# One of four key tiles of the value product as three fp32r passes of a split pair, q projected one unit ahead

## Chip, core and metric

The kernel runs on one core of a Trainium2 chip. The metric is the device time of one execution in microseconds; a shorter time is better. Engines: TensorE (PE, with its weight loads PEld), VectorE (DVE), ScalarE (ACT), GpSimd (POOL) and SyncE (SP), which issues DMAs here.

## The reference

Four layers on x of 2048 tokens by 256: a recurrent time mix, an FFN with low-rank experts, an attention, and an FFN with one of eight experts. Each adds to x what it computes from a layer norm of x. The change is in the attention, 16 heads of 128:

```python
w = codes * jnp.repeat(scales, block_size, axis=0)      # q, k, v, out
q = _mxfp4_matmul(x, wq_codes, wq_scales) + bq
...
scores = jnp.einsum('bqhd,bkhd->bhqk', q, k) / jnp.sqrt(jnp.float32(HEAD_DIM))
attn = jax.nn.softmax(scores, axis=-1)
out = jnp.einsum('bhqk,bkhd->bqhd', attn, v).reshape(B, S, NUM_HEADS * HEAD_DIM)
return _mxfp4_matmul(out, wo_codes, wo_scales) + bo
```

## The kernel before

attention() works on units: a unit u is a head (u // 4) and a block of 512 query tokens (u % 4), 64 units in all. Each unit has four steps c = 0 to 3, and each step takes four key tiles of 128 (KPC = 4, 16 key tiles in all). Every engine runs its own list of instructions over the same steps s = 4u + c, written out by hand, and semaphores tie them together. In step s:

- TensorE: score (L1212), four tiles of keys against 512 queries, each as three fp32r passes (hi by hi, hi by lo, lo by hi; the helper three, L574 to L578); turn_top and spread_top (c = 0) for the maximum of each query; project for q (c = 1), for k (all steps of the last unit of a head); sum_rows (c = 2); weigh (L1241 to L1253), the value product of the step PV = 6 earlier, four tiles, each one fp32 matmul, which the profile records as two instructions; project_out (c = 2, 3); project_v, the values of two heads, in four steps out of 32.
- ScalarE: keep (L1321) copies scores from PSUM to prob, in two halves of two tiles, exp (L1327) of the step SUB = 5 earlier; widen_top (L1333) at c = 0; out_hi (L1340) and project_hi (L1312).
- VectorE: shift (L1380) subtracts the maximum in psum_m from prob, of the step 5 earlier, in two halves; largest (L1390, L1393) keeps the running maximum of the scores; row_max (L1404) at c = 0, fold_top (L1397) at c = 3; project_lo (L1372), out_lo (L1414), the reciprocals (L1410), two output adds (L1426) at c = 2 and 3, take_v (L1435).
- GpSimd: add_up sums the probabilities into acc2, at c = 0 of the summed unit in one operation (L1488), else in two (L1492, L1495), with a last fold at c = 3 (L1500). It sums the step that ScalarE has just exponentiated. It also splits weights into hi and lo (split, L1060 to L1064).
- SyncE loads the next weights as soon as the buffers are split.

The lo part of a value is the value less its hi part, where hi is the value as fp32r. Projections come back through two banks psum_w, in the order of the table jobs; claim() waits until the job two before is taken. The order of VectorE in a step is: shift of half 0, out_lo (c = 2), shift of half 1, largest of half 0, row_max (c = 0), largest of half 1, fold_top (c = 3), project_lo, the reciprocals, the output adds, take_v. That of ScalarE is: out_hi (c = 2), keep and exp of half 0, keep and exp of half 1, widen_top (c = 0), project_hi.

## Time and profile before

| | us |
|---|---|
| median of 3 runs | 2996.99 |
| lowest, highest run | 2992.41, 3002.51 |
| the profiled execution's own time | 2983.7 |
| its span | 2982.0 |
| PE busy | 2791.7 (94%) |
| DVE busy | 1974.7 (66%) |
| ACT busy | 1298.6 (44%) |
| POOL busy | 1454.5 (49%) |

Busy time is the time in which an engine has an instruction in work. Matmuls overlap, so the pace of TensorE is the distance between starts and not the mean of one. The attention runs from about 600 to 2679 us.

### The profile page before, as it was taken

What the parts mean: (1) busy time and instruction counts of PE and PEld (TensorE: products, weight loads), DVE (VectorE), ACT (ScalarE), POOL (GpSimd) and SP (SyncE); (2) the same over time, 40 slices, a digit from 0 to 9 for tenths busy, and PEclk for the clock granted to TensorE, in tenths of its full rate; (3) what the DMA queues carried; (4) which work ended last, traced back from release to release, by engine and by line L of the source; (5) the groups of instructions that cost most, each with busy time, mean ns of one, the idle gap of its engine ahead of it and who ended that gap; (6) DMA issues with size and microseconds to landing.
All of it is one profiled execution on the core that took longest, in us unless ns stands there. A gap on an engine that the chain in (4) does not pass through costs nothing. (4 is left out here: it accounts for less than half of the span.)

```text
span 2982.0 us, 31410 instructions
## 1 busy us (share of the span) xinstructions
PE 2791.7 (94%) x10874; PEld 1856.1 (62%) x10875; DVE 1974.7 (66%) x2412; ACT 1298.6 (44%) x1557; POOL 1454.5 (49%) x782
## 2 busy tenths in 40 slices
PE   5886899889999999999999999999999999987995
PEld 2232677566666667667666766766676676657663
DVE  4478443567777777787777777777777777764211
ACT  1201321245555555555555555455545545541121
POOL 0022230046666666665665666567666655664002
PEclk9888699999999999999999999999999999997997
DMA  2000100110000000000000000000000000006012
GB/s 63 0 0 1 49 0 0 22 27 10 11 8 13 8 4 20 4 8 8 13 9 3 20 8 4 8 13 11 3 9 8 4 1 4 1 10 244 23 44 78
DMA packets 57717, 57.71 MB, mean 19 GB/s; under 512 B 8336, under 2 KB 52624, under 8 KB 57584
## 3 DMA queue, kind: packets, MB, share of 16 engines
q1 hardware_dynamic: 54944, 48.75, 6.1%
q0 software_dynamic: 2640, 7.21, 0.7%
q8 instruction: 80, 1.31, 0.2%
q14 instruction: 53, 0.43, 0.0%
HBM read 45.72 MB, written 10.22 MB: 19 GB/s over the span
## 5 line engine op out<-in xcount | busy, mean ns | idle before, releaser
L1251 PE MATMUL at_psum_o<-at_prob,at_v 128*128 128x512 f32 x2048 | 925.6, 595 | 0.0
L1321 ACT ACTIVATE at_prob<-at_psum_s 128x1024 f32<-128x1024 f32 x512 | 523.6, 1023 | 801.8 <-PE at_psum_s L578 801.8
L1492 POOL TENSOR_TENSOR at_acc<-at_acc,at_prob 128x1024 f32<-128x1024 f32 x192 | 454.7, 2368 | 516.7 <-ACT at_prob L1327 516.4
L1380 DVE TENSOR_TENSOR at_prob<-at_prob,at_psum_m 128x1024 f32<-128x1024 f32 x512 | 604.8, 1212 | 65.4 <-PE at_psum_m L1238 65.4
L1393 DVE TENSOR_TENSOR at_top<-at_psum_s,at_top 128x1024 f32<-128x1024 f32 x448 | 547.2, 1221 | 104.9 <-ACT at_prob L1321 92.3
L1251 PEld LDWEIGHTS at_psum_o<-at_prob,at_v 128*128 128x128 f32 x2048 | 379.2, 190 | 380.4 <-issue 367.8
L1327 ACT ACTIVATE at_prob<-at_prob 128x1024 f32<-128x1024 f32 x512 | 539.0, 1053 | 13.2 <-DVE at_prob L1380 12.9
L1495 POOL TENSOR_TENSOR at_acc<-at_acc,at_prob 128x1024 f32<-128x1024 f32 x192 | 475.0, 2474 | 28.1 <-POOL at_acc L1492 0.9
L576 PE MATMUL at_psum_s<-at_q_hi,at_k_hi 128*128 128x512 f32 x1024 | 429.9, 420 | 2.2 <-DVE at_k_lo L1372 2.2
L578 PE MATMUL at_psum_s<-at_q_hi,at_k_lo 128*128 128x512 f32 x1024 | 402.1, 393 | 0.0
L577 PE MATMUL at_psum_s<-at_q_lo,at_k_hi 128*128 128x512 f32 x1024 | 401.4, 392 | 0.0
L1488 POOL TENSOR_TENSOR at_acc<-at_prob 128x1024 f32<-128x1024 f32 x64 | 151.6, 2369 | 208.6 <-ACT at_prob L1327 207.2
L1426 DVE SCALAR_TENSOR_TENSOR x_tok<-at_psum_w,at_rsum,x_tok 128x256 f32<-128x256 f32 x256 | 112.1, 479 | 178.3 <-PE at_psum_w L578 178.3
L576 PEld LDWEIGHTS at_psum_s<-at_q_hi,at_k_hi 128*128 128x128 f32 x1024 | 192.6, 188 | 50.4 <-DVE at_q_lo L1372 8.8
L577 PEld LDWEIGHTS at_psum_s<-at_q_lo,at_k_hi 128*128 128x128 f32 x1024 | 192.7, 188 | 46.8 <-issue 13.6
L578 PEld LDWEIGHTS at_psum_s<-at_q_hi,at_k_lo 128*128 128x128 f32 x1024 | 192.2, 188 | 44.0
L418 POOL TENSOR_TENSOR tm_read<-tm_r,tm_state 128x2048 f32<-128x2048 f32 x8 | 33.3, 4160 | 217.7 <-DVE tm_state L438 217.7
L576 PE MATMUL at_psum_w<-at_wo_hi,at_oT_hi 128*128 128x256 f32 x256 | 122.9, 480 | 0.0
L576 PE MATMUL at_psum_w<-at_x_hi,at_w_hi 128*128 128x512 f32 x256 | 103.0, 402 | 4.3 <-PEq L62 4.3
L916 ACT ACTIVATE lf_hidden<-lf_psum_h,lf_b 128x512 f32<-128x512 f32 x64 | 41.0, 685 | 146.8 <-PE lf_psum_h L578 146.8
L578 PE MATMUL at_psum_w<-at_x_hi,at_w_lo 128*128 128x512 f32 x256 | 101.8, 398 | 0.0
L577 PE MATMUL at_psum_w<-at_x_lo,at_w_hi 128*128 128x512 f32 x256 | 101.3, 396 | 0.0
(314 smaller groups left out, 3889.0 us busy)
## 6 DMA issues: line engine op xcount, KB each, us to landing
ef_gate_up<-in_ef_gate_up SPq DMA_DIRECT2D x8, 1024.0 KB, 14.0
ef_down<-in_ef_down SPq DMA_DIRECT2D x8, 512.0 KB, 12.7
ef_rows_in<-ef_zeros SPq DMA_DIRECT2D x23, 128.0 KB, 1.8
ef_rows<-ef_rows_in SPq DMA_DIRECT2D x23, 128.0 KB, 2.0
ef_rows_out<-ef_result POOLq DMA_DIRECT2D x23, 128.0 KB, 2.0
x_tok<-in_L_attn_x SPq DMA_DIRECT2D x1, 2048.0 KB, 8.2
lf_w<-in_L_ffn_W SPq DMA_DIRECT2D x2, 1024.0 KB, 6.8
at_codes<-in_at_wq_codes SPq DMA_DIRECT2D x16, 128.0 KB, 2.1
```

What stands on the lines that cost most here:

```text
L576: nc.tensor.matmul(out, a_hi, b_hi, start=start, stop=False, **kw)
L577: nc.tensor.matmul(out, a_hi, b_lo, start=False, stop=False, **kw)
L578: return nc.tensor.matmul(out, a_lo, b_hi, start=False, stop=stop, **kw)
L1251: last = nc.tensor.matmul(psum_o[:], v[:, kt, half], prob[u % 2][:, kt, :], start=(kt == 0), stop=(kt == KT - 1))
L1321: nc.scalar.activation(prob[u % 2][:, c * KPC + 2 * half:c * KPC + 2 * half + 2, :], psum_s[:, 2 * half:2 * half + 2, :], ACT.Copy).then_i ...
L1327: nc.scalar.activation(part, part, ACT.Exp).then_inc(exp_done, 1)
L1380: nc.vector.tensor_tensor(part, part, psum_m[:].unsqueeze(1).to_broadcast([P, 2, BT]), ALU.subtract).then_inc(shifted, 1)
L1393: nc.vector.tensor_tensor(top2[:], part, top2[:], ALU.max).then_inc(maxed, 1)
L1426: last = nc.vector.scalar_tensor_tensor(row, bank(key)[:, bass.ts(j, D)], rsum[:, u % 2, t:t + 1], row, ALU.mult, ALU.add)
L1488: nc.gpsimd.tensor_tensor(acc2[:], first, second, ALU.add).then_inc(summed, 2)
L1492: nc.gpsimd.tensor_tensor(acc2[:], acc2[:], first, ALU.add).then_inc(summed, 1)
L1495: nc.gpsimd.tensor_tensor(acc2[:], acc2[:], second, ALU.add).then_inc(summed, 1)
```

## The change

- The last of the four key tiles of each step (SPLIT = 1, KF = 3) is multiplied as three fp32r passes, with v_hi, v_lo as weights and p_hi, p_lo streamed. The other three stay fp32.
- p_hi is made by ScalarE (split_hi, a copy of 512 columns of prob to fp32r), p_lo by VectorE (split_lo, prob less p_hi), both 256 times. weigh waits for p_lo before its last tile.
- take_v makes v_whole, v_hi and v_lo for that tile, from 256 columns each.
- widen_top goes: spread_top reads a column of row_top with a step of zero as weights.
- q is projected for the next unit (c = 1) instead of for the next head; its buffers hold two blocks. Two q projections move from the first three steps to units 1 and 2.
- The weights of q and k are loaded and split apart, with a semaphore each. The lists of loads on SyncE are reordered: k, v, o, q. GpSimd splits k at step 2 of a head and q at step 10, where it split both at 2.

The diff, cut to its core:

```diff
+SPLIT = 1
...
+    KF = KPC - SPLIT
...
-        if c == 1 and u >= 1 and u - 1 < U - NB:
-            job(("q", (u - 1) // NB + 1, (u - 1) % NB))
+        if c == 1 and u + 1 < U:
+            job(("q", *divmod(u + 1, NB)))
         if s < 3:
             job(("k", 0, s + 1))
-            job(("q", 0, s + 1))
...
+        def split_q(pool, h):
+            pool.wait_ge(qk_loaded[0], (h + 1) * N_QK)
             if h >= 1:
                 pool.wait_ge(w_ready, jobs["q", h - 1, NB - 1] + 1)
-                pool.wait_ge(w_ready, jobs["k", h - 1, NB - 1] + 1)
             nc.gpsimd.tensor_tensor(scales[:, 0], scales[:, 0], factor[:].unsqueeze(2).to_broadcast([P, NC, HD]),
                                     ALU.mult).then_inc(q_factor, 1)
             pool.wait_ge(q_factor, h + 2)
-            split(pool, w_hi[:], codes[:], scales[:], w_lo[:], w_split, h * 3)
+            split(pool, w_hi[:, 0], codes[:, 0], scales[:, 0], w_lo[:, 0], w_split[0], h * 3)
+
+        def split_k(pool, h):
+            pool.wait_ge(qk_loaded[1], (h + 1) * N_QK)
+            if h >= 1:
+                pool.wait_ge(w_ready, jobs["k", h - 1, NB - 1] + 1)
+            split(pool, w_hi[:, 1], codes[:, 1], scales[:, 1], w_lo[:, 1], w_split[1], h * 3)
...
                     for h in range(NH):
...
+                        if h + 1 < NH:
+                            sp.wait_ge(w_split[1], (h + 1) * 3)
+                            load_qk(sp, 1, h + 1)
+                        if h % 2 == 0 and h // 2 + 1 < NH // 2:
+                            sp.wait_ge(wv_split, (h // 2 + 1) * 3)
+                            load_v(sp, h // 2 + 1)
+                        if h >= 1:
+                            sp.wait_ge(wo_split, h * 3)
+                            load_o(sp, h)
+                        if h + 1 < NH:
+                            sp.wait_ge(w_split[0], (h + 1) * 3)
+                            load_qk(sp, 0, h + 1)
...
-                            last = nc.tensor.transpose(psum_m[:, bass.ts(t, P)], wide_top[:, t, :], ident[:])
+                            last = nc.tensor.transpose(psum_m[:, bass.ts(t, P)], row_top[:, t:t + 1].to_broadcast([P, P]), ident[:])
...
-                            last = nc.tensor.matmul(psum_o[:], v[:, kt, half], prob[u % 2][:, kt, :],
-                                                    start=(kt == 0), stop=(kt == KT - 1))
+                            nc.tensor.matmul(psum_o[:], v[:, c, t, half], prob[u % 2][:, c * KPC + t, :],
+                                             start=(c == 0 and t == 0), stop=False)
+                        pe.wait_ge(p_lo_ready, u * CH + c + 1)
+                        slot = (u * CH + c) % 2
+                        for t in range(SPLIT):
+                            last = three(nc, psum_o[:], v_hi[:, c, t, half], v_lo[:, c, t, half],
+                                         p_hi[:, slot, t, :], p_lo[:, slot, t, :],
+                                         start=False, stop=(c == CH - 1 and t == SPLIT - 1))
...
-                    def widen_top(u):
...
+                    def split_hi(u, c):
+                        n = u * CH + c
+                        act.wait_ge(exp_done, 2 * n + 2)
+                        if n >= 2:
+                            act.wait_ge(pv_done, n - 1)
+                        nc.scalar.activation(p_hi[:, n % 2], prob[u % 2][:, c * KPC + KF:(c + 1) * KPC, :],
+                                             ACT.Copy).then_inc(p_hi_ready, 1)
...
+                    def split_lo(u, c):
+                        n = u * CH + c
+                        dve.wait_ge(p_hi_ready, n + 1)
+                        if n >= 2:
+                            dve.wait_ge(pv_done, n - 1)
+                        nc.vector.tensor_tensor(p_lo[:, n % 2], prob[u % 2][:, c * KPC + KF:(c + 1) * KPC, :],
+                                                p_hi[:, n % 2].bitcast(F32), ALU.subtract).then_inc(p_lo_ready, 1)
...
+                            nc.vector.tensor_tensor(v_whole[:, 0:2 - plain, :], psum[:, plain:2, :], wide,
+                                                    ALU.add).then_inc(v_steps, 1)
+                            nc.vector.tensor_tensor(v_hi[:, c, part, :], psum[:, plain:2, :], wide,
+                                                    ALU.add).then_inc(v_steps, 1)
+                            dve.wait_ge(v_steps, m + 2)
+                            made = nc.vector.tensor_tensor(v_lo[:, c, part, :], v_whole[:, 0:2 - plain, :],
+                                                           v_hi[:, c, part, :].bitcast(F32), ALU.subtract)
...
                         if at == 2 and h + 1 < NH:
-                            split_qk(pool, h + 1)
+                            split_k(pool, h + 1)
+                        if at == 10 and h + 1 < NH:
+                            split_q(pool, h + 1)
```

How this moves instructions, at three places of the middle of the attention. VectorE in the steps c = 0 and c = 1 of a unit before: shifts (at_prob), running maxima (at_top), row_max (at_row_top), project_lo (at_q_lo).

```order
L1380 TENSOR_TENSOR at_prob<-at_prob,at_psum_m 128x1024 x2
L1390 COPY at_top<-at_psum_s 128x1024 [waits at_top_ready,at_kept]
L1404 TENSOR_REDUCE at_row_top<-at_psum_w 128x4 [waits at_wide_ready,at_w_ready]
L1393 TENSOR_TENSOR at_top<-at_psum_s,at_top 128x1024 [waits at_maxed,at_kept]
L1380 TENSOR_TENSOR at_prob<-at_prob,at_psum_m 128x1024 [waits at_top_spread]
L1380 TENSOR_TENSOR at_prob<-at_prob,at_psum_m 128x1024
L1393 TENSOR_TENSOR at_top<-at_psum_s,at_top 128x1024 [waits at_maxed,at_kept] x2
L1372 SCALAR_TENSOR_TENSOR at_q_lo<-at_psum_w,at_bias,at_q_hi 128x512 [waits at_hi_ready]
L1380 TENSOR_TENSOR at_prob<-at_prob,at_psum_m 128x1024
```

The same steps of VectorE now:

```order
L1398 TENSOR_TENSOR at_prob<-at_prob,at_psum_m 128x1024 x2
L1408 COPY at_top<-at_psum_s 128x1024 [waits at_top_ready,at_kept]
L1422 TENSOR_REDUCE at_row_top<-at_psum_w 128x4 [waits at_top_spread,at_w_ready]
L1411 TENSOR_TENSOR at_top<-at_psum_s,at_top 128x1024 [waits at_maxed,at_kept]
L1453 TENSOR_TENSOR at_p_lo<-at_prob,at_p_hi 128x512 [waits at_pv_done,at_p_hi_ready]
L1398 TENSOR_TENSOR at_prob<-at_prob,at_psum_m 128x1024 [waits at_top_spread]
L1398 TENSOR_TENSOR at_prob<-at_prob,at_psum_m 128x1024
L1411 TENSOR_TENSOR at_top<-at_psum_s,at_top 128x1024 [waits at_maxed,at_kept] x2
L1390 SCALAR_TENSOR_TENSOR at_q_lo<-at_psum_w,at_bias,at_q_hi 128x512 [waits at_hi_ready]
L1453 TENSOR_TENSOR at_p_lo<-at_prob,at_p_hi 128x512 [waits at_pv_done,at_p_hi_ready]
L1398 TENSOR_TENSOR at_prob<-at_prob,at_psum_m 128x1024
```

A subtraction into at_p_lo with two waits has come to the end of each step, behind row_max and the maxima at c = 0 and behind project_lo at c = 1; before, the next step's shift followed there.

ScalarE in the same two steps before: keep (at_prob from at_psum_s), exp (at_prob from at_prob), widen_top, project_hi (at_q_hi).

```order
L1321 ACTIVATE at_prob<-at_psum_s 128x1024 [waits at_scored]
L1327 ACTIVATE at_prob<-at_prob 128x1024 [waits at_shifted]
L1333 ACTIVATE at_wide_top<-at_row_top 128x512 [waits at_top_spread,at_w_free]
L1321 ACTIVATE at_prob<-at_psum_s 128x1024 [waits at_scored,at_summed,at_pv_done]
L1327 ACTIVATE at_prob<-at_prob 128x1024 [waits at_shifted]
L1321 ACTIVATE at_prob<-at_psum_s 128x1024 [waits at_scored]
L1327 ACTIVATE at_prob<-at_prob 128x1024 [waits at_shifted]
L1312 ACTIVATE at_q_hi<-at_psum_w,at_bias 128x512 [waits at_w_ready]
L1340 ACTIVATE at_oT_hi<-at_psum_o 128x512 [waits at_w_ready,at_pv_done]
```

ScalarE there now:

```order
L1339 ACTIVATE at_prob<-at_psum_s 128x1024 [waits at_scored]
L1345 ACTIVATE at_prob<-at_prob 128x1024 [waits at_shifted]
L1352 ACTIVATE at_p_hi<-at_prob 128x512 [waits at_pv_done,at_exp_done]
L1339 ACTIVATE at_prob<-at_psum_s 128x1024 [waits at_scored,at_summed,at_pv_done]
L1345 ACTIVATE at_prob<-at_prob 128x1024 [waits at_shifted]
L1339 ACTIVATE at_prob<-at_psum_s 128x1024 [waits at_scored]
L1345 ACTIVATE at_prob<-at_prob 128x1024 [waits at_shifted]
L1352 ACTIVATE at_p_hi<-at_prob 128x512 [waits at_pv_done,at_exp_done]
L1330 ACTIVATE at_q_hi<-at_psum_w,at_bias 128x512 [waits at_w_ready]
L1359 ACTIVATE at_oT_hi<-at_psum_o 128x512 [waits at_w_ready,at_pv_done]
```

The copy into at_wide_top is gone, and a copy into at_p_hi follows the second exp of each step; at c = 1 project_hi stands behind it.

TensorE in weigh and the first spreading transpose at c = 0, before:

```order
L1251 MATMUL at_psum_o<-at_prob,at_v 128x512 [waits at_exp_done]
L1251 MATMUL at_psum_o<-at_prob,at_v 128x512
L1251 MATMUL at_psum_o<-at_prob,at_v 128x512 [waits at_exp_done]
L1251 MATMUL at_psum_o<-at_prob,at_v 128x512
L1238 MATMUL at_psum_m<-ident,at_wide_top 128x128 [waits at_shifted,at_wide_ready]
```

TensorE there now:

```order
L1264 MATMUL at_psum_o<-at_prob,at_v 128x512 [waits at_exp_done]
L1264 MATMUL at_psum_o<-at_prob,at_v 128x512
L1264 MATMUL at_psum_o<-at_prob,at_v 128x512 [waits at_exp_done]
L576 MATMUL at_psum_o<-at_p_hi,at_v_hi 128x512 [waits at_p_lo_ready]
L577 MATMUL at_psum_o<-at_p_lo,at_v_hi 128x512
L578 MATMUL at_psum_o<-at_p_hi,at_v_lo 128x512
L1252 MATMUL at_psum_m<-ident,at_row_top 128x128 [waits at_shifted,at_w_free]
```

The fourth fp32 tile has become three passes, the first of which waits for p_lo, and the transpose waits for row_max itself (at_w_free) instead of the copy.

## Rows read from the trace of the kernel before

**Rows 1.** Busy time by stretch: a unit, the attention; clock, DMA, GB/s last
```profile
core 0: us, PE busy (x) PEld busy (x) DVE busy (x) ACT busy (x) POOL busy (x), PEclk, DMA share, GB/s
1501.00:1530.40 29.40, 29.40 (x117) 19.32 (x116) 23.31 (x25) 17.02 (x19) 21.16 (x13) 1.00 0.11 18
700.00:2300.00 1600.00, 1600.00 (x6551) 1085.68 (x6550) 1224.50 (x1341) 874.53 (x996) 1005.96 (x504) 1.00 0.04 9
```

**Rows 2.** Timeline of TensorE, start and duration in us
```profile
1512.24 3.59 PE L1251 MATMUL at_psum_o<-at_prob,at_v 128*128 128x512 f32 x8
1515.27 0.80 PE L576 MATMUL at_psum_s<-at_q_hi,at_k_hi 128*128 128x512 f32 x1
1515.91 0.40 PE L577 MATMUL at_psum_s<-at_q_lo,at_k_hi 128*128 128x512 f32 x1
...
1523.48 0.40 PE L576 MATMUL at_psum_s<-at_q_hi,at_k_hi 128*128 128x512 f32 x1
...
1526.24 3.59 PE L1251 MATMUL at_psum_o<-at_prob,at_v 128*128 128x512 f32 x8
```

**Rows 3.** Groups by form, VectorE then ScalarE, 700 to 2300 us
```profile
L1380 DVE TENSOR_TENSOR at_prob<-at_prob,at_psum_m 128x1024 f32<-128x1024 f32 x398 | 470.3, 1212 | 50.9 <-PE at_psum_m L1238 50.9
L1393 DVE TENSOR_TENSOR at_top<-at_psum_s,at_top 128x1024 f32<-128x1024 f32 x348 | 425.0, 1221 | 77.4 <-ACT at_prob L1321 67.8
L1426 DVE SCALAR_TENSOR_TENSOR x_tok<-at_psum_w,at_rsum,x_tok 128x256 f32<-128x256 f32 x198 | 86.7, 479 | 139.2 <-PE at_psum_w L578 139.2
...
L1372 DVE SCALAR_TENSOR_TENSOR at_q_lo<-at_psum_w,at_bias,at_q_hi 128x512 fp32r<-128x512 f32 x50 | 37.5, 751 | 15.0 <-ACT at_q_hi L1312 15.0
L1414 DVE TENSOR_TENSOR at_oT_lo<-at_psum_o,at_oT_hi 128x512 fp32r<-128x512 f32 x50 | 34.5, 690 | 27.9 <-ACT at_oT_hi L1340 27.9
L1404 DVE TENSOR_REDUCE at_row_top<-at_psum_w 128x4 f32<-128x512 f32 x49 | 33.3, 679 | 0.0
...
L1410 DVE RECIPROCAL at_rsum<-at_psum_w 128x4 f32<-128x4 f32 x50 | 8.6, 172 | 0.0
...
L1333 ACT ACTIVATE at_wide_top<-at_row_top 128x512 f32<-128x512 f32 x49 | 30.8, 628 | 0.0
```

**Rows 4.** Timelines of ScalarE, GpSimd and VectorE around one step
```profile
1526.07 1.05 ACT L1327 ACTIVATE at_prob<-at_prob 128x1024 f32<-128x1024 f32 x1
...
1527.92 1.06 ACT L1327 ACTIVATE at_prob<-at_prob 128x1024 f32<-128x1024 f32 x1
...
1513.73 2.37 POOL L1488 TENSOR_TENSOR at_acc<-at_prob 128x1024 f32<-128x1024 f32 x1 [2.74 <-ACT at_prob L1327]
...
1527.20 2.37 POOL L1492 TENSOR_TENSOR at_acc<-at_acc,at_prob 128x1024 f32<-128x1024 f32 x1 [1.69 <-ACT at_prob L1327]
1529.71 2.68 POOL L1495 TENSOR_TENSOR at_acc<-at_acc,at_prob 128x1024 f32<-128x1024 f32 x1
...
1529.33 0.79 DVE L1397 TENSOR_TENSOR at_top<-at_top 128x512 f32<-128x512 f32 x1
```

**Rows 5.** Timelines: fold_top alone, then with an add
```profile
633.06 0.69 DVE L1397 TENSOR_TENSOR at_top<-at_top 128x512 f32<-128x512 f32 x1
...
1330.90 0.69 DVE L1397 TENSOR_TENSOR at_top<-at_top 128x512 f32<-128x512 f32 x1
...
1330.94 2.92 POOL L1495 TENSOR_TENSOR at_acc<-at_acc,at_prob 128x1024 f32<-128x1024 f32 x1
```

**Rows 6.** Timelines of VectorE and GpSimd in the first layer's scan
```profile
217.16 4.42 DVE L438 TENSOR_TENSOR_SCAN tm_state<-tm_decay,tm_kv 128x2048 f32<-128x2048 f32 x1
...
224.97 5.49 DVE L438 TENSOR_TENSOR_SCAN tm_state<-tm_decay,tm_kv 128x2048 f32<-128x2048 f32 x1
...
221.67 4.51 POOL L418 TENSOR_TENSOR tm_read<-tm_r,tm_state 128x2048 f32<-128x2048 f32 x1 [6.17 <-DVE tm_state L438]
```

**Rows 7.** TensorE's timeline and a stretch at the attention's end
```profile
2673.96 1.84 PE L1260 MATMUL at_psum_w<-at_ones,at_acc 128*128 128x1 f32 x8 [3.52 <-POOL at_acc L1500]
...
2674.00:2678.00 4.00, 4.00 (x19) 4.00 (x20) 0.85 (x3) 0.00 (x0) 0.00 (x0) 0.50 0.00 0
```

More of the change, by code:

```diff
@@ L1158, in attention @@
             halves = {key: n for n, key in enumerate(k for k in jobs if k[0] in "qk")}
+            split_jobs = [n for n in range(KT // 2) if 2 * n % KPC + 2 > KF]
+            v_split_jobs = len(split_jobs)
+            v_split_index = {n: i for i, n in enumerate(split_jobs)}
             def bank(key):
@@ L1354, in _ @@
                                 exp(eu, ec, half)
-                        if c == 0 and 1 <= u <= U:
-                            widen_top(u - 1)
-                        if c == 1 and u >= 1 and u - 1 < U - NB:
-                            project_hi(0, (u - 1) // NB + 1, (u - 1) % NB)
+                        if 0 <= eu < U:
+                            split_hi(eu, ec)
+                        if c == 1 and u + 1 < U:
+                            project_hi(0, *divmod(u + 1, NB))
                         if s < 3:
                             project_hi(1, 0, s + 1)
-                            project_hi(0, 0, s + 1)
                         if u % NB == NB - 1 and u < U - 1:
@@ L1459, in _ @@
                                 fold_top(u)
-                        if c == 1 and u >= 1 and u - 1 < U - NB:
-                            project_lo(0, (u - 1) // NB + 1, (u - 1) % NB)
+                        if c == 1 and u + 1 < U:
+                            project_lo(0, *divmod(u + 1, NB))
                         if s < 3:
                             project_lo(1, 0, s + 1)
-                            project_lo(0, 0, s + 1)
                         if u % NB == NB - 1 and u < U - 1:
                             project_lo(1, u // NB + 1, c)
+                        if 0 <= eu < U:
+                            split_lo(eu, ec)
                         if c == 2 and 2 <= u < U + 2:
```

102 lines of the change are left out of this document (47 added, 55 removed).

## The prediction

> **What bounds the kernel now.** I read the busy time by stretch first, then TensorE's timeline, then VectorE's groups, then the three other engines around one step. From 700 to 2300 us TensorE is busy 1600 of 1600 us at granted clock 1.00 [rows 1]: the attention is its stage. A unit (one head, 512 query tokens, four steps) without projections of keys or values takes 29.4 us, in which VectorE is busy 23.31 and GpSimd 21.16. I call it a plain unit. Its timeline gives the passes. Twelve fp32r passes of a score step run from 1523.48 to 1526.24, 0.230 each; the eight records of four fp32 tiles run from 1512.24 to one pass before 1515.91, 3.44 us, or 0.86 a tile [rows 2].
>
> **TensorE: what is removed.** One tile of each of 256 steps goes from 0.86 to 3 x 0.230 = 0.69, so 0.17 x 256 = 43 us of work go, and a plain unit would need 28.7. [...]
>
> Around it: q projections keep their number; two of them (1.4 us each) move from the first steps, where TensorE waited for k_lo, into steps where it doesn't, and half of that comes back, +1.4 us. widen_top leaves ScalarE; the spreading transposes read row_top with a zero step. No row has such a weight load; ScalarE read the same broadcast in 0.63 us [rows 3], no longer than VectorE takes for 512 columns (0.69), so I take 0, and at worst a few tenths for 64 units. The weight loads of q and k are split into two visits of SP and GpSimd with the same bytes; q's DMAs now stand behind the wait for the o split on SP and have over ten steps before they are used: 0.
>
> **ScalarE and VectorE: what is added.** 256 split_hi of 512 columns, 0.63 each like widen_top [rows 3], put ScalarE from 17 to about 19 us of a unit: hidden. 256 split_lo on VectorE: unhindered, 0.69 [rows 5], less 0.08 that neighbours overlap. Four make VectorE's own work 23.3 + 2.5 = 25.8; with its waits for ScalarE in step c = 1 and for kept halves I count 27.3. That alone still fits under 28.7. Of every second value bank one tile is split: its take becomes four operations of 256 columns, about 0.4 each (the 256-column output adds take 0.48 [rows 3]), so a value step has 0.69 + 1.6 = 2.3 us on VectorE, where TensorE has 2.9 us of projection.
>
> **What split_lo collides with.** It reads two SBUF operands (prob and p_hi), and GpSimd's adds read two as well. The trace of before has three such meetings. fold_top (top2 with top2) takes 0.69 alone [rows 5], but 0.79 when it starts 0.24 us before L1492 ends (1527.20 + 2.37 = 1529.57) [rows 4]. A GpSimd add started 0.04 after it takes 2.92 instead of 2.37 [rows 5]. The scan of the first layer takes 4.42 alone and 5.49 when it starts 1.21 before GpSimd's product ends (221.67 + 4.51) [rows 6]. Each time the second operation is held for what is left of the first, less 0.14. Shifts and maxima, which have one operand in PSUM, keep 1.21 and 1.22 whatever GpSimd does [rows 3]. The Trainium skill (SBUF — State Buffer, Who interferes with whom) says that a VectorE instruction with two SBUF inputs and a GpSimd instruction that reads SBUF exclude each other, the later one for the whole of the earlier; the trace agrees up to a hold of 1.07 us, and has none longer.
>
> So the phase decides. In step c = 3 exp0 starts at 1526.07, L1492 at +1.13, L1495 at +3.64; exp1 ends at 1528.98, +2.91 [rows 4]. split_hi ends near +3.6, when L1495 starts. VectorE has a row_max, a fold or an out_lo ahead of split_lo in three of four steps and comes later than that: it finds GpSimd at the start of a 2.37 us add.
>
> **The walk**, in us from the first shift of a step, once VectorE is the late one from the durations of [rows 3, 4]: shifts to 2.34; exp0 1.29 to 2.34; L1492 2.42 to 4.8; L1495 4.93 to 7.3; maxima to 4.82; exp1 to 4.2; p_hi at 4.95.
> - c = 0: row_max puts the end of the maxima at 5.4; split_lo held until 7.3, done 7.85; next shift 7.8.
> - c = 1: GpSimd has one add here, 0.13 after exp1 (like the one at 1513.73), 4.37 to 6.74. project_hi now stands behind split_hi, so project_lo ends at 6.4; split_lo done 7.3; 7.25.
> - c = 2: out_lo between the shifts; split_lo from 5.55 held to 7.3, done 7.85; reciprocal and two adds of output rows to 8.8.
> - c = 3: fold holds L1495 until about 7.8; it waits already when fold ends at 5.56, so split_lo is held until 7.8, done 8.4; two output adds, 9.2.
>
> Sum 33.05, where VectorE without holds has 27.3 and TensorE 28.7. The next unit begins alike, so it is the period: +3.65 on 29.4. Behind it TensorE becomes the waiting engine, first at spread_top, which waits for row_max, and at score, which waits for the maxima.
>
> Units: 64, of which 15 carry k projections. There TensorE has 5.6 us more, project_lo fits into the held time, and both need 34 to 35: +0.5 each, +8. Seven carry a pair of heads' values: VectorE has about 2.3 us more in each of four steps, TensorE 2.9: +2 each, +14. That leaves 41 plain ones (one is the fill): 41 x 3.65 = +150. The tail has no scores to hide split_hi and split_lo: +4, with the fill's 1.4, +5. Sum +177. The TensorE work removed (43) is inside these, since the new period is VectorE's. 2983.7 + 177 = 3161 for the profiled execution; the median of the runs shown is 13.3 above it, so I forecast **3174 us**, 6% slower.
>
> The bounds: if no hold is longer than the longest seen, 1.07, the holds are 1.07 + 0.25 + 1.07 + 1.07 = 3.5 and the unit 30.8, +1.4 x 41 = +57: about 3054. If near ties go to VectorE in one step of four, its hold of 1.75 goes: 31.3, +1.9 x 41, with the rest 3100.
>
> **Rivals.**
> - *Faster: split_lo goes in ahead of the second add.* Place: the start of L1495 against the end of split_hi, some 0.1 us apart. If VectorE is there first, GpSimd is held for 0.5, which it can afford (21 of 29), nothing is held on VectorE, and TensorE stays the bound: -43 + 1.4 + 3 for the tail = -38, 2959. For it: in c = 2 the maxima end about when p_hi comes. Against: in c = 0 and c = 3 VectorE is busy until 0.4 and 0.7 after L1495's start, and two holds of 2 us already make 27.3 + 4 = 31.3 over 28.7. It decides only if holds stay under 28.7 - 27.3 = 1.4 us a unit. [...] Chance 0.12, with all other ways to no lasting hold.
> - *Holds end early*, capped at 1.07: 3054. Chance 0.06.
> - *TensorE's clock falls too.* In the walk TensorE waits some 3.4 us at spread_top in each unit. After the one wait of 3.52 us in the tail, the next 4 us ran at granted 0.50, the 1.2 GHz level [rows 7]. Were that so in each plain unit, up to 4 us of its work would take twice as long, and of the 4.3 us that TensorE has over, little is left: up to +2 x 41 = +80, 3255. Chance 0.04.
> - *No difference*: holds of just about 1.4 to 2 us a unit, which eat the 43 us: 0.02.
>
> **How the numbers follow.** The forecast case has 0.76. About 9 us, 0.3%, is what a measurement can tell from no change. Faster 0.12, same 0.02, slower 0.86. The forecast's own range is 3080 to 3230 (periods of 31.4 to 34.4 us); taking in the capped holds below and most of the clock case above gives 3040 to 3250, and leaves out the faster case and the rest, under 0.2.
>
> **What would show it.** split_lo's mean near 2 us instead of 0.69, with the short ones in the steps with the single add; VectorE near 95% busy in the attention where it had 77%; TensorE's busy share down, with waits for at_p_lo, row_top and maxima; a plain unit of 33 us. The forecast is wrong if split_lo averages under about 1.0 us, or if TensorE is still busy without gaps; its size is off if the hold is there but the phase of the adds another.

## The result: 4.6% slower, and the profile after

| | before | after |
|---|---|---|
| median of the runs, us | 2994.7 (4 runs, 2989.8 to 3002.5) | 3132.7 (4 runs, 3126.9 to 3140.2) |
| span of the profiled execution, us | 2982.0 | 3125.2 |

The ratio is 1.046, 95% interval 1.0431 to 1.049. The time is 41 us under the forecast of 3174 and inside the range. The busy shares and two stretches after, in the columns of [rows 1] (the attention, and a plain unit):

```profile
PE 2802.0 (90%) x11130; PEld 1932.3 (62%) x11131; DVE 2451.6 (78%) x2764; ACT 1444.6 (46%) x1749; POOL 1524.5 (49%) x830
...
700.00:2300.00 1600.00, 1512.96 (x6386) 1079.73 (x6385) 1503.61 (x1525) 931.91 (x1079) 993.39 (x503) 0.98 0.04 9
1588.00:1620.00 32.00, 31.70 (x118) 22.13 (x118) 29.36 (x29) 18.70 (x23) 20.97 (x12) 0.90 0.02 7
```

TensorE had no gap in the attention [rows 1]; now it is idle for 87 of 1600 us, and VectorE is busy 1504 of 1600, 94%, where it had 1224.5. The groups of VectorE and GpSimd for the same stretch, beside [rows 3]:

```profile
L1398 DVE TENSOR_TENSOR at_prob<-at_prob,at_psum_m 128x1024 f32<-128x1024 f32 x374 | 441.2, 1209 | 0.0
L1411 DVE TENSOR_TENSOR at_top<-at_psum_s,at_top 128x1024 f32<-128x1024 f32 x329 | 400.9, 1218 | 18.5 <-ACT at_prob L1339 4.2
L1453 DVE TENSOR_TENSOR at_p_lo<-at_prob,at_p_hi 128x512 fp32r<-128x512 f32 x187 | 365.8, 1956 | 0.4 <-ACT at_p_hi L1352 0.3
...
L1541 POOL TENSOR_TENSOR at_acc<-at_acc,at_prob 128x1024 f32<-128x1024 f32 x140 | 358.3, 2559 | 20.6 <-POOL at_acc L1538 0.9
L1538 POOL TENSOR_TENSOR at_acc<-at_acc,at_prob 128x1024 f32<-128x1024 f32 x141 | 337.9, 2397 | 441.8 <-ACT at_prob L1345 441.8
```

split_lo (L1453) takes 1.96 us in the mean for 512 columns, though an operation of that size takes 0.69 alone [rows 5]. The time over 0.69 I call its hold. Shifts and maxima, with one operand in PSUM, keep their 1.21 and 1.22. Shifts no longer wait for anything, where they had 50.9 us of waits for TensorE in [rows 3]. The timelines of VectorE's split_lo and fold_top and of GpSimd, over one plain unit (start and duration in us):

```profile
1588.99 2.66 DVE L1453 TENSOR_TENSOR at_p_lo<-at_prob,at_p_hi 128x512 fp32r<-128x512 f32 x1
...
1598.17 1.11 DVE L1453 TENSOR_TENSOR at_p_lo<-at_prob,at_p_hi 128x512 fp32r<-128x512 f32 x1
...
1604.90 0.69 DVE L1453 TENSOR_TENSOR at_p_lo<-at_prob,at_p_hi 128x512 fp32r<-128x512 f32 x1 [0.29 <-ACT at_p_hi L1352]
...
1612.18 0.81 DVE L1415 TENSOR_TENSOR at_top<-at_top 128x512 f32<-128x512 f32 x1
1612.91 2.89 DVE L1453 TENSOR_TENSOR at_p_lo<-at_prob,at_p_hi 128x512 fp32r<-128x512 f32 x1
```

```profile
1588.74 2.36 POOL L1541 TENSOR_TENSOR at_acc<-at_acc,at_prob 128x1024 f32<-128x1024 f32 x1
...
1596.36 2.37 POOL L1534 TENSOR_TENSOR at_acc<-at_prob 128x1024 f32<-128x1024 f32 x1 [3.57 <-ACT at_prob L1345]
...
1604.94 2.92 POOL L1541 TENSOR_TENSOR at_acc<-at_acc,at_prob 128x1024 f32<-128x1024 f32 x1
...
1612.58 2.67 POOL L1541 TENSOR_TENSOR at_acc<-at_acc,at_prob 128x1024 f32<-128x1024 f32 x1
```

Put the two side by side. At 1588.99 split_lo starts 0.25 after an add that ends at 1591.10; without a hold it would take 0.69, and it ends at 1591.65, so its work began at 1590.96, 0.14 before the add's end. At 1598.17 the single add has 0.56 left, and split_lo takes 1.11 = 0.69 + 0.42, again 0.14 less than what was left. At 1604.90 split_lo starts 0.04 ahead of the add: it takes 0.69, and the add pays (2.92). At 1612.91 the add itself had been held by fold_top, and split_lo is held for 2.2 us, twice the longest hold in the trace before. The whole trace goes by this: 222 of the 256 split_lo start inside a two-input operation of GpSimd, and each is held for what is left of it less 0.09 to 0.15 us (0.14 in 212 of them).

TensorE's waits from 700 to 2300 us (total, times, longest), and its timeline at the first wait of this unit:

```profile
PE at_psum_m L1252 <- DVE at_row_top L1422: 42.5, 17, 2.7
PE at_psum_w L576 <- DVE x_tok L1444: 18.6, 17, 2.5
PE at_psum_o L1264 <- DVE at_oT_lo L1432: 14.9, 16, 1.1
PE at_psum_w L576 <- DVE at_rsum L1428: 11.1, 6, 1.8
```

```profile
1587.99 1.12 PE L1252 MATMUL at_psum_m<-ident,at_row_top 128*128 128x128 f32 x4 [2.70 <-DVE at_row_top L1422]
1588.76 0.78 PE L576 MATMUL at_psum_s<-at_q_hi,at_k_hi 128*128 128x512 f32 x1
1589.34 0.63 PE L577 MATMUL at_psum_s<-at_q_lo,at_k_hi 128*128 128x512 f32 x1
1589.76 0.63 PE L578 MATMUL at_psum_s<-at_q_hi,at_k_lo 128*128 128x512 f32 x1
```

Everything it waits for comes from VectorE. After the wait of 2.70 us its passes start 0.42 apart instead of 0.23: half the clock, as in [rows 7] (granted 0.50 from 1588 to 1594 us). The granted clock of the unit is 0.90, that of the attention 0.98.

**The units.** I take a unit's length from one first maximum (L1408, before L1390) to the next. All 63 such lengths, and what lies around them, make up the 143.2 us between the two spans. In the last column stands the forecast for the same units.

| group | before, each | after, each | sum, us | forecast, us |
|---|---|---|---|---|
| 28 plain units | 29.39 | 12 of 32.8, 1 of 32.65, 15 of 30.8 to 31.5 | +72.1 | +102 |
| 14 k units | 34.96 | 33.3 | -22.4 | +7 |
| 7 pairs of units with values | 70.07 | 78.7 (40.8 + 37.9) | +60.7 | +40 |
| units 60 to 62 | 29.39, 27.95, 27.96 | 32.8 | +13.1 | +11 |
| units 0 to 3 | | | +2.1 | +8 |
| before the first (-1.1), behind the last maximum (+18.6) | | | +17.5 | +9 |

### The profile page after: what moved, and what is told of

It reads as the page before. It is cut to its first block and busy times, and to the rows that moved or that the text cites. A ratio compares the mean times of both kernels' runs of the same rounds, so it can differ in the third digit from the quotient of the medians.

```text
span 3125.2 us, 32974 instructions
## 1 busy us (share of the span) xinstructions
PE 2802.0 (90%) x11130; PEld 1932.3 (62%) x11131; DVE 2451.6 (78%) x2764; ACT 1444.6 (46%) x1749; POOL 1524.5 (49%) x830
## 5 line engine op out<-in xcount | busy, mean ns | idle before, releaser
L1538 POOL TENSOR_TENSOR at_acc<-at_acc,at_prob 128x1024 f32<-128x1024 f32 x192 | 459.7, 2394 | 587.9 <-ACT at_prob L1345 587.9
L1264 PE MATMUL at_psum_o<-at_prob,at_v 128*128 128x512 f32 x1536 | 709.9, 598 | 26.0 <-DVE at_oT_lo L1432 24.1
L1453 DVE TENSOR_TENSOR at_p_lo<-at_prob,at_p_hi 128x512 fp32r<-128x512 f32 x256 | 501.8, 1960 | 8.9 <-ACT at_p_hi L1352 8.6
L1541 POOL TENSOR_TENSOR at_acc<-at_acc,at_prob 128x1024 f32<-128x1024 f32 x192 | 492.8, 2567 | 28.1 <-POOL at_acc L1538 0.9
L1264 PEld LDWEIGHTS at_psum_o<-at_prob,at_v 128*128 128x128 f32 x1536 | 283.1, 190 | 287.8 <-issue 233.6
L576 PE MATMUL at_psum_s<-at_q_hi,at_k_hi 128*128 128x512 f32 x1024 | 416.6, 407 | 5.5 <-DVE at_k_lo L1390 5.0
L577 PE MATMUL at_psum_s<-at_q_lo,at_k_hi 128*128 128x512 f32 x1024 | 410.2, 401 | 0.0
L578 PE MATMUL at_psum_s<-at_q_hi,at_k_lo 128*128 128x512 f32 x1024 | 409.1, 400 | 0.0
L576 PEld LDWEIGHTS at_psum_s<-at_q_hi,at_k_hi 128*128 128x128 f32 x1024 | 198.9, 194 | 44.5 <-DVE at_k_lo L1390 6.5
L576 PE MATMUL at_psum_o<-at_p_hi,at_v_hi 128*128 128x512 f32 x256 | 202.7, 792 | 0.1
L1352 ACT ACTIVATE at_p_hi<-at_prob 128x512 fp32r<-128x512 f32 x256 | 161.7, 632 | 8.1
L418 POOL TENSOR_TENSOR tm_read<-tm_r,tm_state 128x2048 f32<-128x2048 f32 x8 | 33.3, 4161 | 217.6 <-DVE tm_state L438 217.6
L1444 DVE SCALAR_TENSOR_TENSOR x_tok<-at_psum_w,at_rsum,x_tok 128x256 f32<-128x256 f32 x256 | 111.4, 475 | 13.1 <-PE at_psum_w L578 7.6
```

The costliest lines, as they stand in the source:

```text
L576: nc.tensor.matmul(out, a_hi, b_hi, start=start, stop=False, **kw)
L577: nc.tensor.matmul(out, a_hi, b_lo, start=False, stop=False, **kw)
L578: return nc.tensor.matmul(out, a_lo, b_hi, start=False, stop=stop, **kw)
L1264: nc.tensor.matmul(psum_o[:], v[:, c, t, half], prob[u % 2][:, c * KPC + t, :], start=(c == 0 and t == 0), stop=False)
L1352: nc.scalar.activation(p_hi[:, n % 2], prob[u % 2][:, c * KPC + KF:(c + 1) * KPC, :], ACT.Copy).then_inc(p_hi_ready, 1)
L1453: nc.vector.tensor_tensor(p_lo[:, n % 2], prob[u % 2][:, c * KPC + KF:(c + 1) * KPC, :], p_hi[:, n % 2].bitcast(F32), ALU.subtract).then_i ...
```

## The experiments

Eleven more kernels ran, each beside runs of the kernel before, whose median was 2984.0 to 2984.8 us each time. Diffs are against the change. These medians of before lie 10 us under the 2994.7 of the table above, so I compare a run with the change by its ratio; the first four expectations in microseconds were written before that was known.

**1. The rest of the change alone.** SPLIT's tile goes back to fp32, with no hi and lo parts of probabilities and values. What stays is the order of projections and loads, and the spreading without widen_top.

```diff
-    KF = KPC - SPLIT
+    KF = KPC
...
-                            split_hi(eu, ec)
...
-                            split_lo(eu, ec)
```

> All of the change except the split tile: four fp32 tiles in weigh, no split_hi, split_lo or split values; q is projected one unit ahead, the loads are reordered, the spreading transposes read row_top with a zero step. Port theory and load theory: nothing of it costs, 2995 to 3002 us (the moved q projections +1.4). Rival that the reordering or the zero-step weight load is what costs: 3050 or more, with TensorE waiting at at_psum_m or for at_w_free.

Measured: 2987.2 us, ratio 1.001 (0.9999 to 1.0021), and TensorE busy 1600 of 1600 us. The rest is free, as the prediction had it, to 0.2%; the loss is the split tile's.

**2. split_lo left out.**

```diff
-                        pe.wait_ge(p_lo_ready, u * CH + c + 1)
+                        pe.wait_ge(p_hi_ready, u * CH + c + 1)
...
-                                          p_hi[:, slot, t, :], p_lo[:, slot, t, :],
+                                          p_hi[:, slot, t, :], p_hi[:, slot, t, :],
...
-                            split_lo(eu, ec)
```

> The change without split_lo: weigh waits for p_hi and streams it in place of p_lo, so the lo part of the probabilities is left out of the product. TensorE's passes, split_hi and the split values stay. Port theory and load theory: VectorE is back at 23.3 of a plain unit of 28.7 us, so the TensorE gain shows: 2950 to 2965. Rival that the passes on TensorE, its clock or ScalarE's work cost: stays over 3000.

Measured: 2943.7 us, ratio 0.9871 (0.9849 to 0.9894), and TensorE busy without a gap. So 40 us are to be had from the passes. split_lo costs the difference of the ratios, 1.046 to 0.987, or some 176 us.

**3. and 4. split_lo's second input, and GpSimd's inputs.** In one kernel split_lo becomes an operation of its size that reads one operand; in the other split_lo is whole and GpSimd's sums only write, so the row sums are left out.

```diff
-                        nc.vector.tensor_tensor(p_lo[:, n % 2], prob[u % 2][:, c * KPC + KF:(c + 1) * KPC, :],
-                                                p_hi[:, n % 2].bitcast(F32), ALU.subtract).then_inc(p_lo_ready, 1)
+                        nc.vector.tensor_reduce(p_lo[:, n % 2, 0], prob[u % 2][:, c * KPC + KF, :].unsqueeze(2), AX.X,
+                                                ALU.max).then_inc(p_lo_ready, 1)
```

> split_lo replaced by an operation of VectorE of the same 512 columns, the same place and the same waits, that reads one SBUF operand (a maximum over groups of one), so p_lo holds a copy of prob and the product is another. Port theory: about 0.7 us each, never held, GpSimd's adds at 2.37 to 2.40, a plain unit of 28.7 to 29.0, total 2950 to 2975. Load theory (256 more operations in VectorE's list and their waits for ScalarE are enough): 3100 to 3135, as with the change.

```diff
-                            nc.gpsimd.tensor_tensor(acc2[:], acc2[:], second, ALU.add).then_inc(summed, 1)
+                            nc.gpsimd.memset(acc2[:], 1.0).then_inc(summed, 1)
```

(and the same for the other three sums.)

> The change with split_lo whole, but GpSimd's adds of probabilities only write ones (the row sums are left out): no GpSimd instruction of the loop reads SBUF except the weight splits. Port theory: split_lo at 0.69 but for steps with weight splits (mean 0.7 to 0.8), total 2950 to 2965. Load theory: as with the change, 3100 to 3135, split_lo at 0.7 but VectorE without a pause.

Measured: 2954.5 us, ratio 0.9906 (0.9887 to 0.9926), and 2949.2 us, ratio 0.9877 (0.9858 to 0.9895). The group of split_lo in the first and in the second, with the second's sum and the first's:

```profile
L1453 DVE TENSOR_REDUCE at_p_lo<-at_prob 128x512 fp32r<-128x512 f32 x204 | 138.2, 677 | 5.0 <-ACT at_p_hi L1352 5.0
...
L1541 POOL TENSOR_TENSOR at_acc<-at_acc,at_prob 128x1024 f32<-128x1024 f32 x153 | 382.0, 2496 | 22.5 <-POOL at_acc L1538 0.9
```

```profile
L1453 DVE TENSOR_TENSOR at_p_lo<-at_prob,at_p_hi 128x512 fp32r<-128x512 f32 x203 | 148.3, 731 | 1.1 <-ACT at_p_hi L1352 0.8
...
L1541 POOL MEMSET at_acc<- 128x1024 f32 x152 | 144.8, 953 | 132.9 <-ACT at_prob L1345 132.2
```

One more VectorE operation per step, with all of its waits and in the same place, costs next to nothing in plain units (28.7 in the mean) and 11 us in all against experiment 2: what costs is that it reads two operands in SBUF beside GpSimd operations that read. The second kernel's sums are also shorter, so alone it would show less than the first does.

**5. Preparations kept, the tile in fp32** (it reads the values of the step's first tile, so the product is another).

```diff
-                            last = three(nc, psum_o[:], v_hi[:, c, t, half], v_lo[:, c, t, half],
-                                         p_hi[:, slot, t, :], p_lo[:, slot, t, :],
-                                         start=False, stop=(c == CH - 1 and t == SPLIT - 1))
+                            last = nc.tensor.matmul(psum_o[:], v[:, c, 0, half], prob[u % 2][:, c * KPC + KF + t, :],
+                                                    start=False, stop=(c == CH - 1 and t == SPLIT - 1))
```

> The change with all preparations (split_hi, split_lo, split values, the wait for p_lo), but the fourth tile multiplied as one fp32 matmul with the weights of tile 0 of the step (p_hi, p_lo and the split values are not used). It takes TensorE's saving away: 43 us of passes come back. Port theory: where VectorE sets the period the time hardly moves; value steps and steps with k projections gain or lose a little: 3130 to 3155. Rival that TensorE is still the bound and lost time by other means: 43 us more, 3170 to 3180.

Measured: 3136.0 us, ratio 1.0514 (1.0496 to 1.0531), split_lo at 1.93 us. The ratio is 0.5% over the change's 1.046, some 16 us, where 43 us of work would be 1.4%: with VectorE as the bound, most of what TensorE saves is worth nothing.

**6. split_lo on GpSimd**, behind its own adds, in the same step.

```diff
-                        nc.vector.tensor_tensor(p_lo[:, n % 2], prob[u % 2][:, c * KPC + KF:(c + 1) * KPC, :],
+                        nc.gpsimd.tensor_tensor(p_lo[:, n % 2], prob[u % 2][:, c * KPC + KF:(c + 1) * KPC, :],
```

> split_lo moved to GpSimd, behind its adds of the same step; nothing left out. About 1.3 us each there. GpSimd goes from 18 to 23.4 us of a plain unit of 28.7. Port theory: VectorE is held only at fold_top, TensorE is the bound again in plain units: 2955 to 2975, with some waits for p_lo where GpSimd splits weights of values and outputs in one step (5 to 6 us of it). Load theory of VectorE: the same sign. Rival that p_lo comes too late from GpSimd: 3000 and more, waits of TensorE for at_p_lo.

Measured: 2989.9 us, ratio 1.0009 (0.9994 to 1.0024). The expected 2955 to 2975 missed. split_lo takes 1.29 us there, most plain units are at 28.67, and still nothing is won. TensorE's waits from 700 to 2300 us name one thing, six times; then GpSimd's timeline ahead of one of them:

```profile
PE at_psum_o L576 <- POOL at_p_lo L1521: 19.1, 6, 3.2
```

```profile
926.40 1.31 POOL L1521 TENSOR_TENSOR at_p_lo<-at_prob,at_p_hi 128x512 fp32r<-128x512 f32 x1
927.67 1.27 POOL L1064 TENSOR_TENSOR at_wv_hi<-at_v_codes,at_v_scales 128x512 fp32r<-128x512 f32 x1
...
933.72 2.41 POOL L1536 TENSOR_TENSOR at_acc<-at_acc,at_prob 128x1024 f32<-128x1024 f32 x1
...
939.93 1.26 POOL L1521 TENSOR_TENSOR at_p_lo<-at_prob,at_p_hi 128x512 fp32r<-128x512 f32 x1
```

Between two rest parts lie six weight splits (927.67 to 933.76), since at step 8 of every second head GpSimd splits the values' and the outputs' weights together. The rest part comes late, TensorE waits 3.2 us for it, and such units take 32 to 35 us. I had expected these waits, but put 5 to 6 us of GpSimd's work on them and not 3.2 us of TensorE's waiting six times over, with units longer by 3.5 to 6.

**7. split_lo on VectorE one step later**, right behind the second shift.

```diff
+                        if 0 <= pu < U:
+                            split_lo(pu, pc)
...
-                        if 0 <= eu < U:
-                            split_lo(eu, ec)
```

> split_lo stays on VectorE, whole, but one step later, right behind the second shift, some 2.3 us into the step, when GpSimd's second add of the step before is over and its first of this step is about to start; nothing left out. Port theory: mostly no hold, split_lo 0.69 to 1.0 in the mean, GpSimd's first add held by up to 0.5, total 2955 to 2985. Load theory (the work and not the phase): 3100 or more, since VectorE has exactly the work of the change.

Measured: 3043.6 us, ratio 1.0198 (1.0181 to 1.0215), a miss: I had expected at most 2985. Both groups of two-input operations on VectorE, 700 to 2300 us:

```profile
L1453 DVE TENSOR_TENSOR at_p_lo<-at_prob,at_p_hi 128x512 fp32r<-128x512 f32 x193 | 188.9, 979 | 0.0
L1415 DVE TENSOR_TENSOR at_top<-at_top 128x512 f32<-128x512 f32 x49 | 139.2, 2840 | 1.7
```

split_lo is nearly free now, but fold_top, with 0.72 in the change, takes 2.84. At 1524.48 it starts 0.11 after an add (1524.37). I had placed the one operation and not asked what its going would do to the next one of its kind.

**8. As 6, with the values' weights split five steps later.**

```diff
-                        if at == 8 and h % 2 == 0 and h // 2 + 1 < NH // 2:
+                        if at == 13 and h % 2 == 0 and h // 2 + 1 < NH // 2:
```

> As the run with split_lo on GpSimd behind its adds, but GpSimd's split of the value weights (split_v) moved from step 8 of an even head to step 13, so that it no longer shares a step with the split of the output weights. Nothing is left out; the output is the reference's. Theory (what ate the gain in that run was six to seven units in which the rest part came late behind two weight splits in one step, 3.2 us of TensorE wait each): the waits of TensorE for at_p_lo in those units go, they come down from 32 to 35 us to about 28.7, and the time is 2950 to 2970 us, ratio 0.984 to 0.990, faster than both kernels. Rival (GpSimd as a whole is short of time, so the lateness only moves to step 13): the waits turn up there and the time stays 2980 to 2995 us.

Measured: 2958.0 us over 6 runs, ratio 0.9896 (0.9878 to 0.9914): faster than both kernels. The same stretch:

```profile
700.00:2300.00 1600.00, 1600.00 (x6896) 1146.73 (x6895) 1272.85 (x1445) 1000.92 (x1172) 1296.69 (x756) 1.00 0.04 9
```

TensorE is busy without a gap again, and every plain unit takes 28.64 to 28.67 us. The collision of two weight splits in one step was what had eaten the gain of 6.

**9. GpSimd's sums as operations that read one operand.** The row sums are left out by it.

```diff
-                            nc.gpsimd.tensor_tensor(acc2[:], acc2[:], second, ALU.add).then_inc(summed, 1)
+                            nc.gpsimd.tensor_scalar(acc2[:], second, 1.0, None, ALU.add).then_inc(summed, 1)
```

(and the same for the other two of 1024 columns.)

> The change with the folded sums on GpSimd as operations that read one operand in SBUF and write one (a number added in place of the second operand); the row sums are left out by it, the rest stands. Theory (two-input work of VectorE and reads of SBUF by GpSimd exclude each other, whatever number of operands GpSimd reads): split_lo still shows held instances, its mean well over 0.73 us, up to the length of the GpSimd operations; if those take 1.6 to 2.4 us the plain unit is 30 to 32 us and the time 3030 to 3130 us. Rival (only GpSimd's two-input operations take the shared path): split_lo is 0.69 to 0.73 us as with the writes-only run, the plain unit 28.7 us and the time 2950 to 2960 us.

Measured: 2962.1 us, ratio 0.9917 (0.99 to 0.9933), so the theory of the expectation missed. But its rival is not the whole truth either: split_lo's mean is 0.76 us, and some are held. VectorE's split_lo and the GpSimd operations beside it:

```profile
712.12 1.38 DVE L1453 TENSOR_TENSOR at_p_lo<-at_prob,at_p_hi 128x512 fp32r<-128x512 f32 x1
720.77 0.68 DVE L1453 TENSOR_TENSOR at_p_lo<-at_prob,at_p_hi 128x512 fp32r<-128x512 f32 x1
728.91 0.80 DVE L1453 TENSOR_TENSOR at_p_lo<-at_prob,at_p_hi 128x512 fp32r<-128x512 f32 x1
```

```profile
711.92 2.77 POOL L1541 TENSOR_SCALAR at_acc<-at_prob 128x1024 f32<-128x1024 f32 x1 [0.15 <-POOL at_acc L1538]
...
718.32 2.77 POOL L1534 TENSOR_SCALAR at_acc<-at_prob 128x1024 f32<-128x1024 f32 x1 [2.24 <-ACT at_prob L1345]
...
728.12 2.77 POOL L1541 TENSOR_SCALAR at_acc<-at_prob 128x1024 f32<-128x1024 f32 x1 [0.15 <-POOL at_acc L1538]
```

A split_lo that starts 0.20 after such an operation is held until 0.89 after its start (712.12 + 1.38 - 0.69 = 712.81), one that starts 0.79 after it until 0.90. One that starts in the middle (720.77, with 0.32 left) isn't held at all. The whole trace agrees: 303 split_lo and fold_top start inside such an operation, and none that starts 1.0 us or more after it is held. So this operation of GpSimd, which reads one operand, keeps VectorE out for its first 0.9 us of 2.77 only. Whether that goes by the one operand or by the kind of operation (tensor_scalar) isn't told apart.

**10. A long split_lo that can't be held**: one reduction with one input, over three tiles. The rest part isn't computed.

```diff
-                        nc.vector.tensor_tensor(p_lo[:, n % 2], prob[u % 2][:, c * KPC + KF:(c + 1) * KPC, :],
-                                                p_hi[:, n % 2].bitcast(F32), ALU.subtract).then_inc(p_lo_ready, 1)
+                        nc.vector.tensor_reduce(p_lo[:, n % 2, 0],
+                                                prob[u % 2][:, c * KPC + 1:(c + 1) * KPC, :].rearrange("p t n -> p n t"),
+                                                AX.X, ALU.max).then_inc(p_lo_ready, 1)
```

> The change with split_lo replaced by one long reduction on VectorE that reads one operand in SBUF (three tiles of the probabilities, 1536 elements, written over one tile); the rest part is therefore not computed, its place, waits and signals stand. A held split_lo and a long one occupy VectorE alike, so this gives a length of 1.5 to 2.1 us in every step without any hold. Theory (what costs is VectorE's time per step, not the exclusion as such): VectorE's stretch of the plain unit is 20.2 us of the other work and 4 of these, 26 to 29 us, about the mean of the change, and the time 3040 to 3130 us. Rival (the cost is the exclusion itself, GpSimd's late adds and row sums with it): the time stays under 3000 us though VectorE is as busy as in the change.

Measured: 3089.2 us, ratio 1.034 (1.0313 to 1.0367).

```profile
L1453 DVE TENSOR_REDUCE at_p_lo<-at_prob 128x512 fp32r<-128x1536 f32 x191 | 368.1, 1927 | 0.0
```

At 1.93 us in each of four steps most plain units take 31.25, so all else in one takes 31.25 - 7.7 = 23.5. In the change the four take 2.73 + 1.15 + 2.52 + 2.87 = 9.27 in a unit of 32.8: 23.5 again. This gives the price in one line: a plain unit takes at least 23.5 us plus its four split_lo, and at least TensorE's 28.67. The break is near 5.2 us for four, 1.3 each. It is a floor: plain units of the change with one or two short split_lo lie up to 1.8 us above it, and there VectorE waits more for the other engines (up to 2.6 us of a unit, where it has 1.1 in the others).

**11. Only the order made sure.** GpSimd's last add of a step waits for split_lo of the same step.

```diff
+                            pool.wait_ge(p_lo_ready, u * CH + c + 1)
                             nc.gpsimd.tensor_tensor(acc2[:], first, second, ALU.add).then_inc(summed, 2)
...
+                            pool.wait_ge(p_lo_ready, u * CH + c + 1)
                             nc.gpsimd.tensor_tensor(acc2[:], acc2[:], second, ALU.add).then_inc(summed, 1)
```

> The change with nothing moved and nothing left out; only GpSimd's last add of each step (the second of two, or the single one) waits until VectorE's split_lo of the same step is done, so that VectorE always comes first where the two used to collide. The output is the reference's. Theory (the time lost is VectorE held by a GpSimd add that started just before): split_lo falls to a mean of 0.69 to 0.85 us, fold_top keeps 0.69 to 0.8, GpSimd's adds stay at 2.37 and start up to 2 us later, which its 8 us of idle time in a unit take; the plain unit is 28.7 us, TensorE 100% busy from 700 to 2300 us, and the time 2945 to 2970 us, ratio 0.983 to 0.990, faster than both kernels. Rival (the late adds hold the next shift-side work: the first add of the next step, the freeing of the probabilities or the row sums come late, or the late add now meets fold_top or out_lo): ScalarE's keep waits for summed or fold_top is held, the unit stays over 29.5 us and the time over 3000 us.

Measured: 2960.4 us over 5 runs, ratio 0.9923 (0.991 to 0.9937). Two waits turn 4.6% slower into 0.8% faster. That is less than the ratio of 0.983 to 0.990 that I had expected: TensorE still waits 7.2 us of the stretch, and split_lo and fold_top, at 0.86 and 0.97, are over the means I gave. Stretch and groups:

```profile
700.00:2300.00 1600.00, 1592.76 (x6856) 1140.01 (x6855) 1422.93 (x1639) 998.23 (x1167) 1028.61 (x547) 1.00 0.04 9
```

```profile
L1543 POOL TENSOR_TENSOR at_acc<-at_acc,at_prob 128x1024 f32<-128x1024 f32 x152 | 364.8, 2400 | 199.9 <-DVE at_p_lo L1453 197.8
...
L1453 DVE TENSOR_TENSOR at_p_lo<-at_prob,at_p_hi 128x512 fp32r<-128x512 f32 x202 | 174.1, 862 | 4.3 <-ACT at_p_hi L1352 2.4
...
L1415 DVE TENSOR_TENSOR at_top<-at_top 128x512 f32<-128x512 f32 x50 | 48.4, 969 | 1.7
```

GpSimd now idles 197.8 us ahead of the last of two adds, 1.3 us each, and as much ahead of the single ones, and hardly anybody misses it. Some units still show a hold of up to 2.3 us, by the first add of a step: split_lo at 1512.82 finds one that started at 1512.13, right behind a weight split that had kept GpSimd until then. Experiments 8 and 11 have intervals that overlap, so I don't rank them.

## Why the prediction was right, and where its size was off

**The mechanism is shown, from both sides.** Take away split_lo's second input (3), or GpSimd's reads (4), or the bad order (11), and split_lo goes back to 0.68 to 0.86 us and TensorE to 99.5% or more. Put an equal length in its place without any exclusion (10), and most of the loss comes back: ratio 1.034 against 1.046, where experiment 2 has 0.987. The Trainium skill (SBUF — State Buffer, Who interferes with whom) has the rule; the rows bear it out for GpSimd operations with two inputs, with holds of 2.2 us, twice as long as the trace before could show. What the prediction calls "less 0.14" is 0.14 for VectorE's operations; for the add that fold_top held [rows 5] it is 0.10, 0.65 left and 0.55 longer.

**Signs named ahead.** split_lo near 2 us: 1.96. VectorE near 95%: 94%. Waits of TensorE for row_top: 42.5 us, the largest. A short one in the step with the single add: 1.11. A plain unit of 33: 32.8 where all steps are held. The waits for maxima and for at_p_lo that I named are not among the four of the list: TensorE waits instead for output rows, reciprocals and out_lo. By experiment 5 most of the gain of 43 us is hidden under VectorE's period; 1 puts the rest of the change at no more than 0.2%.

**The step that failed: 41 plain units at 33.05.** The walk took the end of split_hi and the start of GpSimd's second add as fixed in every unit. In 15 of 28 plain units at least one near tie, at c = 0 or c = 2, goes to VectorE; a hold of about 1.8 us goes with it, and the unit takes 30.8 to 31.5. I had that as a bound (31.3 for each) and not as part of the forecast, and it makes these 28 units 30 us too dear. Nor are these ties left to chance. GpSimd and VectorE in such a unit, at c = 2:

```profile
1086.69 0.74 POOL L1067 TENSOR_TENSOR at_w_lo<-at_codes,at_w_hi 128x256 fp32r<-128x256 f32 x1
1087.38 2.37 POOL L1538 TENSOR_TENSOR at_acc<-at_acc,at_prob 128x1024 f32<-128x1024 f32 x1
1089.89 2.92 POOL L1541 TENSOR_TENSOR at_acc<-at_acc,at_prob 128x1024 f32<-128x1024 f32 x1
...
1089.87 0.68 DVE L1453 TENSOR_TENSOR at_p_lo<-at_prob,at_p_hi 128x512 fp32r<-128x512 f32 x1
```

The split of q's weights, which the change moved to step 10 of a head, keeps GpSimd until both adds are late, and split_lo is first by 0.02 us. Of the 15 units 14 are the third of their head, where this split stands, and all such units among the 28 are in it; in 12 of them c = 2 is won, in the other two c = 0, right behind the split of the outputs' weights. The third unit of the last head has no such split: it is held in all four steps and takes 32.85. The prediction put the two visits for q and k at 0 by their bytes, and its walk had no weight split in it. No run places the q split elsewhere, so this is read from the trace and not tested.

Where all four are held, the walk was right to 0.3 us, in part by luck: it gave the four split_lo 2.45 + 0.9 + 2.3 + 2.84 = 8.5 us where 9.27 was measured, and the rest of the unit 24.6 us where 23.5 was. The unit shown above is an exception: it wins the tie at 1604.90 by 0.04 us and still takes 32.65. VectorE waits 0.85 us ahead of its output adds there, for a TensorE that began the unit at half clock; that this is the clock's doing is argued, not shown.

**k units, +0.5 each, were -1.6.** In the change one of these reads [1.73, 0.68, 1.72, 2.03] for its four split_lo, 6.2 us instead of 9.3: project_lo stands between the maxima and split_lo and takes the place of a hold. With 23.5, and 3.0 for four project_lo (0.749 each), that is 32.7, against 33.3 measured. I had held TensorE's 34 to be a floor; it isn't one for this length, which is below the 34.27 of experiment 8, because a unit is cut at VectorE's maxima. TensorE has no gap in these units, and in the ones right behind them it waits 0 to 1.1 us, where it waits 2.4 to 3.8 in the next: it seems to catch up there, which wasn't tried. These units took 29 us less than forecast. The four misses (30 and 29 us too much, 21 and 8 too little) leave 30 of the 34 us between the sum of 177 and the 143 measured.

**Value pairs, +5.7 each with the second unit's 3.65, were +8.7.** I set VectorE's extra work against TensorE's, as if they ran side by side. They do so only in part. The operations of take_v take 56 us for 6 pairs, 9.4 a pair, and the pair takes 13.1 more than two plain units of 32.8. The other 4 us are waits: in a pair VectorE is idle for 5.8 to 7.4 us, where two plain units have 2.2. In the pair from 862.6 to 941.9 us it waits for TensorE's projection of the values four times, 5.0 us in all:

```profile
DVE at_v L1466 <- PE at_psum_w L578: 5.0, 4, 1.7
```

TensorE itself waits 5.2 us there, 1.85 and 2.53 of it right ahead of these projections: the two engines wait in turn. In all the pairs took 21 us more than forecast.

**Behind the last maximum, +9 with the fill, was +17.5.** Of the 18.6 us there, 10.1 lie inside the attention, from the last first maximum to the last output add (59.8 before, 69.9 now): a last unit at VectorE's pace and a tail in which split_hi and split_lo have no cover. The other 8.5 lie in the last layer, whose instructions are unchanged (302.5 before, 311.0 now, but 302.5 in experiment 11). In that layer TensorE stands still for 2.9 us ahead of 2894.33, without anything that the profile shows, the nine passes behind it start 0.43 us apart instead of 0.23, and it then waits 1.9 us for VectorE; the traces of before and of the other runs have no such gap there. That makes up some 6.6 of the 8.5 us, in this one execution; its cause stays open.

**The rivals.** The faster one (split_lo first, 2959) had a chance of 0.12 and didn't come by itself; 11 makes it true by force. That both times are near 2960 is luck: the rival's is 0.987 of the time before it, that of 11 is 0.992. Capped holds are refuted by the hold of 2.2. A falling clock is there, but small: granted 0.98 over the attention and 0.90 in a unit, where I had put up to 80 us on it; the waits for row_top that pull it down are 17 of at most 2.7 us, and not one of 3.4 in every unit. Two of the bounds are also added up wrongly: 3054 for the capped holds and 3080 for the range leave out the 27 us of k units, value pairs and tail that the forecast's sum has; with them they are 3081 and 3106.

## What to carry to other kernels

Before an operation with two SBUF inputs goes to VectorE, list GpSimd's operations with two SBUF inputs that run in the same time. Its price is its length plus what is left of the one it finds (less 0.14 us here), so look at who starts first and by how much, not at busy shares: here 0.69 us of work in a step with plenty of room cost 2. If GpSimd has time to spare, make it wait by a semaphore for the short operation of VectorE; two such lines turned a ratio of 1.046 into 0.992 here. And after removing one hold, look at the next two-input operation on the list, which may take its place (7).
